# Two expert blocks with per-token heads woven in: first slot's down products summed step by step, bank lanes, heads in quarters, gates as a stage

## The reference, cut to what matters

```python
x = x + _L0_ffn_ref(_layernorm(x, axis=-1), ...)      # experts, first pass (k = 0)
x = x + _L0_attn_b_ref(_layernorm(x, axis=-1), ...)   # heads of one token
x = x + _L0_ffn_ref(_layernorm(x, axis=-1), ...)      # experts, second pass (k = 1)
x = x + _L1_attn_a_ref(_layernorm(x, axis=-1), ...)   # delta rule

# experts: per token the two best of E = 8 experts, one "slot" each
logits = x @ Wg.T
probs = jax.nn.softmax(logits); rw, sel = jax.lax.top_k(probs, K); rw = rw / rw.sum(...)
for k in range(K):                                    # slot k
    x1 = base1 + lora1;  x3 = base3 + lora3           # 896 wide
    x2 = jax.nn.silu(x1) * x3
    down = x2 @ W2.T                                  # beside it a2_all, 256 wide too
    out = out + (down + lora2) * rw[:, k:k + 1]

# heads of one token: 16 heads of 16 numbers, each token for itself
scores = jnp.einsum('bshd,bstd->bsht', q, k) / jnp.sqrt(jnp.float32(HD))
weights = jax.nn.softmax(scores, axis=-1)
attn = jnp.einsum('bsht,bstd->bshd', weights, v)
```

## Time and profile before

| | us |
|---|---|
| median of 3 runs | 1569.86 |
| lowest, highest | 1567.25, 1571.34 |
| the profiled execution | 1570.56 |
| its span | 1568.8 |
| PE busy, share | 1311.2, 84% |
| DVE busy, share | 746.1, 48% |
| ACT busy, share | 419.9, 27% |
| mean granted TensorE clock | 0.89 |

### The profile page before, as it was taken

One profiled execution on the slowest core, in us unless ns is written; L12 is line 12 of the kernel. 1 busy time (PEld: TensorE's weight loads), 2 busy tenths in 40 slices (PEclk: granted clock), 3 DMA queues, 4 the chain that ended last, 5 costly groups with the idle time before them and its releaser, 6 DMA issues.

```text
span 1568.8 us, 17406 instructions
## 1 busy us (share of the span) xinstructions
PE 1311.2 (84%) x6780; PEld 998.9 (64%) x6780; DVE 746.1 (48%) x1631; ACT 419.9 (27%) x910; POOL 79.6 (5%) x69
## 2 busy tenths in 40 slices
PE   5689987986988798877877999879779887897878
PEld 4567563744857678665666766547458576786656
DVE  4533286585445454224233335855943453633241
ACT  2522020111322241334242521111113222413251
POOL 0000000000110110000000000000001102100000
PEclk9889998997999779689987999979979998896898
DMA  9000000000000000000000000000000000000000
GB/s 377 3 1 0 0 1 0 0 1 0 1 1 1 1 1 1 0 1 1 7 8 1 1 0 1 1 0 0 0 0 1 1 0 1 1 1 1 1 1 14
DMA packets 3264, 16.97 MB, mean 11 GB/s; under 512 B 240, under 2 KB 2288, under 8 KB 2544
## 3 DMA queue, kind: packets, MB, share of 16 engines
q10 hardware_dynamic: 1008, 13.77, 2.1%
q1 hardware_dynamic: 2176, 2.10, 0.4%
HBM read 14.82 MB, written 1.05 MB: 10 GB/s over the span
## 4 chain that ended last, share of the span: by engine, by line
PE 61%; DVE 25%; ACT 8%; issue 4%; POOL 1%; DMA 0%; DVEq 0%; ACTq 0%; POOLq 0%
PE bank L612 56%; DVE scr L1657 4%; ACT scr L1167 3%; DVE scr L1658 2%; DVE scr L1641 2%; DVE scr L1640 2%; PE bank L619 2%; DVE scr L1697 1%; PE bank L987 1%; DVE scr L1583 1%; ACT scr L1145 1%; DVE stat L1424 1%; DVE X L1417 1%; DVE scr L1625 1%; POOL rstd L1956 1%
## 5 line engine op out<-in xcount | busy, mean ns | idle before, releaser
L612 PE MATMUL bank<-pack,scr 128*128 128x256 f32 (+2 forms) x944 | 339.1, 515 | 5.2 <-ACT scr L1145 5.2
L612 PE MATMUL bank<-XnT,pack 128*128 128x256 f32 x1024 | 273.6, 412 | 17.7 <-ACT XnT L1145 10.6
L612 PEld LDWEIGHTS bank<-pack,scr 128*128 128x128 f32 x944 | 191.1, 209 | 138.1 <-issue 111.6
L612 PE MATMUL bank<-scr,pack 128*128 128x256 f32 x944 | 242.1, 399 | 30.7 <-DVE scr L1583 25.5
L612 PEld LDWEIGHTS bank<-XnT,pack 128*128 128x128 f32 x1024 | 208.7, 208 | 57.0 <-ACT XnT L1145 13.7
L612 PEld LDWEIGHTS bank<-scr,pack 128*128 128x128 f32 x944 | 186.0, 200 | 63.0 <-DVE scr L1583 28.7
L1145 ACT ACTIVATE scr<-bank 128x512 f32<-128x512 f32 (+7 forms) x112 | 49.0, 454 | 284.6 <-PE bank L619 182.9
L1583 DVE TENSOR_TENSOR scr<-bank,scr 128x256 f32<-128x256 f32 x112 | 45.7, 422 | 165.7 <-ACT scr L1214 165.1
L619 PE MATMUL bank<-pack,scr 128*128 128x128 f32 x232 | 43.1, 319 | 89.1 <-DVE scr L1609 25.0
L1417 DVE TENSOR_TENSOR X<-bank,X 128x512 f32<-128x512 f32 x32 | 22.1, 692 | 185.6 <-PE bank L612 185.5
L612 PE MATMUL bank<-scr 32*128 32x128 f32 (+4 forms) x944 | 101.7, 374 | 8.6 <-DVE scr L1871 4.7
(11 more groups left out here) (175 smaller groups left out, 1462.9 us busy)
## 6 DMA issues: line engine op xcount, KB each, us to landing
pack<-pack_dram ACTq DMA_DIRECT2D x1, 6408.0 KB, 17.9
pack<-pack_dram ACTq DMA_DIRECT2D x1, 2052.0 KB, 30.4
pack<-pack_dram ACTq DMA_DIRECT2D x1, 1595.0 KB, 25.0
pack<-pack_dram ACTq DMA_DIRECT2D x1, 1361.0 KB, 7.4
X<-x SPq DMA_DIRECT2D x4, 256.0 KB, 7.9
pack<-pack_dram ACTq DMA_DIRECT2D x1, 1024.0 KB, 20.0
out_dram<-X SPq DMA_DIRECT2D x4, 256.0 KB, 2.1
pack<-pack_dram ACTq DMA_DIRECT2D x1, 657.5 KB, 26.0
```

Source lines behind the costliest of these rows:

```text
L612: return pe.matmul(o, l, r, start=start, stop=stop, skip_group_check=True)
```

## The change

- **Down sums in the loop.** A new stage `down_sum` stands behind each `x_second` in blocks A and B. It takes the first slot's slice m as soon as it is there and adds its product to two open banks, one for each token half. The `down` stages of slot 0 then issue nothing on PE. In the second slot's `down` the wait for each slice's drained bank stands ahead of that slice's matmul and no longer ahead of all.
- **Bank lanes.** While `weave` is set (from the start of `middle` to the end of block B's `spread`), `x_first` and `down` take banks 0 to 2 only, `down_sum` 3 and 4, all else 5 to 7.
- **Heads in quarters.** `HP = 4`: 16 pieces over 1024 numbers in place of 8 over 2048, in more slots of the loop. `heads_in` and the norm stand one step earlier.
- **Layout of the values.** `bV` is stored with the heads innermost, so that line 1657's multiply reads both operands in a row; ACT's copy writes it so.
- **Gates as a stage.** The gates leave `router` and become a stage of their own behind `spread` or `x_first`; `router` and `lora` move out of the block, `spread_t` stands behind them, and `norm_x` now stands behind `x_first` and `gates`.
- **Convolutions.** In the delta rule two of b's convolution pairs stand one level earlier.

```diff
@@
+HP = 4
...
-            v, o = part(s, o, [NT, NH, HD]); bV.append(v)
+            v, o = part(s, o, [NT, HD, NH]); bV.append(v)
...
             return (pw[s][:, a, hh].unsqueeze(2).broadcast_to([P, n, HD, NH]),
-                    bV[s][:, a].rearrange("p t d -> p d t").unsqueeze(1).broadcast_to([P, n, HD, NH]))
+                    bV[s][:, a].unsqueeze(1).broadcast_to([P, n, HD, NH]))
...
         def lanes(name, k, s):
 
+            if weave[0]:
+                return dict(x_first=range(0, 3), down=range(0, 3), down_sum=range(3, 5)).get(name, range(5, 8))
             if not halves[0]:
...
-            for other in (("scores", 0, (d, 0)), ("spread_t", 0, c), ("spread", 0, c)):
+            for other in (("scores", 0, (d, 0)), ("spread_t", 0, c), ("spread", 0, c), ("gates", 0, c)):
...
         def middle(stage, a, b):
 
+            weave[0] = True
             stage("x_first", 0, (b, 0))
             stage("lora", 0, a)
             stage("norm_x", 2, a)
             experts(stage, 0, b, token_heads(a))
+            stage("router", 1, a)
+            stage("lora", 0, b)
             stage("spread_t", 1, a)
-            stage("lora", 0, b)
             stage("spread", 1, a)
+            stage("x_first", 1, (a, 0))
+            stage("gates", 1, a)
             stage("norm_x", 2, b)
-            stage("x_first", 1, (a, 0))
             experts(stage, 1, a, token_heads(b))
+            stage("router", 1, b)
+            stage("lora", 1, a)
             stage("spread_t", 1, b)
-            stage("lora", 1, a)
             stage("spread", 1, b)
+            weave[0] = False
+            stage("x_first", 1, (b, 0))
+            stage("gates", 1, b)
             stage("norm_x", 4, a)
-            stage("x_first", 1, (b, 0))
...
-                             5: [("norm_t", 4, b), ("delta_gate", 0, b)] + conv_(b, 0),
-                             6: conv_(b, 1) + [("delta_log", 0, b)]})
-            for other in [("delta_u", 0, a)] + conv_(b, 2) + [
-                    ("delta_s", 0, a), ("delta_g1", 0, b), ("delta_v", 0, a), ("delta_tok", 0, b), ("delta_o", 0, a),
+                             5: [("norm_t", 4, b), ("delta_gate", 0, b)] + conv_(b, 0, 1),
+                             6: conv_(b, 2) + [("delta_log", 0, b)]})
+            for other in [
+                    ("delta_u", 0, a), ("delta_s", 0, a), ("delta_g1", 0, b), ("delta_v", 0, a), ("delta_tok", 0, b), ("delta_o", 0, a),
...
-            beside = {1: [("norm_t", 2, s)], 2: [("heads_in", 0, s)] + pieces[0:1]}
-            for i in range(1, 7):
-                beside[2 + i] = pieces[i:i + 1]
-            beside["down00"] = pieces[7:8]
+            beside = {0: [("norm_t", 2, s)], 1: [("heads_in", 0, s)]}
+            slots = [1, "f2", 2, "f3", 3, "f4", 4, "f5", 5, "f6", 6, 7, 7, 8, 8, "down00"]
+            for slot, piece in zip(slots, pieces):
+                beside.setdefault(slot, []).append(piece)
             beside["down10"] = [("head_out_t", 0, s), ("head_out", 0, s), ("norm_x", 3, s)]
-            beside["down11"] = [("norm_t", 3, s), ("router", 1, s)]
+            beside["down11"] = [("norm_t", 3, s)]
...
                     stage("x_second", k, (s, m - 2))
+                    if weave[0]:
+                        stage("down_sum", k, (s, m - 2))
...
+                if ("down", r, i, a) in ring.at:
+                    return
                 o = claim(pe, ("down", r, i, a))
-                if i == 1 and a == 0:
-                    for m in range(FT):
+                for m in range(FT):
+                    if i == 1 and a == 0:
                         wait_drained(pe, ("x", r, m))
...
+            def down_sum(k, sm):
+                s, m = sm
+                r = (k, s)
+                wd = w3("m_down", FT)
+                pe.wait_ge(x2_first[s], nth(s, 2 * FT, k * FT + m + 1))
+                for a in range(NT):
+                    o = claim(pe, ("down", r, 0, a)) if m == 0 else bank[ring.bank(("down", r, 0, a))]
+                    last = mm(o[:, :], x2T[s][:, 0, m, a * P:(a + 1) * P], wd[:, m, :], m == 0, m == FT - 1)
+                    if m == FT - 1:
+                        last.then_inc(full[ring.bank(("down", r, 0, a))], 1)
...
-                move(key, bV[s][:, :, :, :].rearrange("p a h d -> p (a h d)"), psum(key, NT * D))
+                move(key, bV[s][:, :, :, :].rearrange("p a d h -> p a h d"), psum(key, NT, NH, HD))
...
                 ins.then_inc(onehot_ready[s], 1)
 
+            def gates(k, s):
+                iota = w("iota")
                 dve.wait_ge(top_exp[s], nth(s, 2, k + 1))
...
-                hh = slice(h * NH // 2, (h + 1) * NH // 2)
+                hh = slice(h * NH // HP, (h + 1) * NH // HP)
```

32 lines of the change are left out of this document (16 added, 16 removed).

## The result

The changed kernel takes 1586.7 us (median; 1584.9 to 1587.3) against 1569.6 for the kernel before. The ratio is 1.0108, with a 95% interval of 1.0091 to 1.0126: **17 us or 1.1% slower**. The forecast was slower, by 28 us. The profiled execution took 1586.82, with a span of 1585.0 against 1568.8: 16.2 us to account for.

The account below looks back on a forecast made before the run. Blocks A and B were taken as DVE-bound. Block A +8.5, block B +4.6 and ahead of C +1.5 make 14.6 a middle; two give 29.2, less 1.2: +28 us, 1598, own range 1590 to 1606, wide range 1574 to 1616.

Parts of the forecast that it names:

- DVE's waits: Blocks A and B: DVE's waits for ACT's silu or exponential total 14.0 us a block, +9.7 over before.
- The loop's own wait: Slices 3 and 5: x_first needs the bank that DVE's second product of slice m-3 frees; DVE waits 1.7 us.
- the low clock behind it: Slices 4 and 6: PE's 3.6 us idle is followed by a low clock, x_first taking 1.8 us longer.
- clock up (1584): Rival: the 3.6 us idle leaves PE's clock up, 3.6 us less a block, 14.4 in all: 1584, chance 0.16.
- DVE's work: Blocks A and B: quarter pieces, row-wise mix reads and unpaired silu products together change DVE's work by -1.6 us a block.
- H: The start of the head projections on PE in a block; for block B it was to move by -3.5 us.
- A to B: Seam between blocks A and B: x_first of slice 0 ends 5.9 us earlier, norm_t waits 5.4 us; net -3.5 us.
- Ahead of C: Seam ahead of block C: -5.9 us, then +5.2 to norm_t and +2.2 for low clock: +1.5 us.
- Small moves: Elsewhere: earlier maxima and later gates in sequence c's first pass, -1.2 us once; convolution pairs in the delta rule, 0.
- The faster one: Rival: the bank loop doesn't bite, 1559, chance 0.12; the change gains if extra DVE waits stay below 2.7 us a block.
- A clock that swings all through the loop: Rival: x_first of slices 3 and 5 also slow, 1.8 us each, 3.6 a block: 1612, chance 0.10.
- The layout at the full rate: Mix multiply reads bV in a row, 1.22 us a quarter; rival that the layout doesn't help: 1619, chance 0.03.

Follow-up runs that it names:

- layout_alone: The kernel before with only bV stored with its 16 heads in a row, so the mix multiply reads both operands in a row: 1529.6 us.
- exp_later: The changed kernel with ACT's exponential of a token row one piece later in ACT's queue, DVE's order unchanged: 1561.8 us.
- layout_exp_seam: The kernel before with the bV layout, the later exponential, lora_t ahead of router and gates behind x_first 0, norm in its old place: 1489.9 us.

## Why the prediction was right, and where its sizes were off

The direction and the mechanism came as forecast. The size did not: 17 us for 28, and 1586.7 lies in the wide range but outside the forecast's own, 1590 to 1606.

**The bound.** Right. Blocks A and B hang on DVE; shortening DVE's work by 5.37 us shortens the stretch by 5.37 us in all four (layout_alone).

**DVE's waits.** The loop was right, and it was the point on which the forecast turned. The forecast's waits add up to 14.0 us a block; 14.1, 13.0, 13.0 and 14.0 were measured. The loop's own wait was put at 1.7 and is 1.91; PE's idle ahead of slices 4 and 6 was put at 3.6 and is 3.46, all eight times. **The term of these stretches that was mis-sized is the low clock behind it**: I took 1.8 us in all eight cases, from the row behind 3.90 us of idle. It came in four, and added 2.8, 1.7, 1.7 and 2.8 us to the waits: 9.0 us where the sum had 14.4. That the waits of a block fit so well is partly luck: without the clock they are 11.3 us where I had 10.5, which takes back 3.2 of those 5.4. And that 1587 lies between my two cases, clock low (1598) and clock up (1584), isn't owed to the half of low clocks alone. It moves the forecast by 5.4 us, to 1593; the rest came from places outside the loop.

**DVE's work.** Put at -1.6 us a block. From H to the end the blocks grew by 7.9, 6.8, 6.8 and 7.8 us for 8.1; less the added waits as measured that leaves -1.8. A quarter operation is 1.22 us, as worked out.

**The seams.** A to B: the way from the last normalization of A to H of B was to shrink by 3.5 us, and went from 43.9 to 40.3 and from 47.6 to 43.4, 3.6 and 4.2. `x_first` of slice 0 was to end 5.9 us earlier and ends 5.3 earlier (counted from `norm_t` 3, first seam): the idle ahead of `lora_t` fell to 1.32 us as worked out, but half of this `x_first` still ran at the low clock. The wait of `norm_t`, put at 5.4, is 5.26; the two rows ahead of and behind it:

```profile
291.96 0.42 DVE L1609 TENSOR_TENSOR scr<-bank,scr 128x256 f32<-128x256 f32 x1 [4.19 <-ACT scr L1238]
...
295.84 0.86 DVE L1456 TENSOR_SCALAR scr<-X,mv,rstd 128x256 f32<-128x256 f32 x2 [0.81 <-POOL rstd L1982]
```

```profile
296.76 1.12 PE L630 MATMUL bank<-pack,scr 128*128 128x128 f32 x4 [5.26 <-DVE scr L1456]
```

Ahead of C I had +1.5 twice; the first gave +1.2, the second -1.4. There the kernel before had run an `x_first` at a low clock and the changed one only its first half, which I had seen but left out of the sum.

**Small moves.** c's region gained 2.8 us for 1.2; the gates' 5.56 us stood ahead of more than the scores' maxima. I haven't taken that apart. The delta rule was put at 0. The idle ahead of `delta_base`'s level went as weighed up (5.89 us to 2.65 and 0.57), the masks' wait came (3.87 us), and they cancel to 0.8 us; but behind it b's delta rule ran at the low clock for 20.5 us where it had been 27.3, which is 3.4 us less, and **no term stood for it**: the whole stretch up to c's router gave 4.8 us where I had put nothing. What turned the clock there I haven't taken apart.

**The sum.** The blocks and seams gave 21.9 for 29.2 (DVE's waits and work 3.0 less, the seams 0.8, C 3.2), c 1.6 less, the delta rules and the rest 2.9 less: 11.8 us, which is 28 less 16.2. So three quarters of the miss lie outside the stretches that the forecast turned on.

**The rivals.** The faster one, decided at 2.7 us of extra waits a block, was far off: the extra waits were 8.6 to 9.7. "A clock that swings all through the loop" had the Trainium skill's page "TensorE: Matmul & The Clock Gate" (section "A second HAM failure mode: psum-queue depth-cycling") behind it; no run shows it: behind the idles of 0.4 to 0.9 us at slices 3 and 5, and of 1.19 us at 4 and 6 in exp_later, the clock never fell. My own ground against it was weak, though: the idle of 4.4 us lies as far back from 284.70, where the clock was up, as from 1172.06, where it was low. The layout at the full rate, for which the Trainium skill's page "SBUF — State Buffer" (section "Door 1: The DMA port swizzle") stood, came: 1.22 us for a quarter and 2.29 for a half, where the old stride took 1.90 and 3.63.

What the forecast did not see is the size of what was on offer: it priced the layout at 5.4 us a block, as work of DVE, and not that PE's idle at the tail goes with it. In the changed kernel that doesn't matter, since the idle stays. It did in every better version.

## What to carry over

Before cutting the banks of a stage into lanes, follow the ring once around: which engine frees the bank, what stands in its queue ahead of the freeing instruction, and whether that engine then waits for what the bank lets start; a fourth bank, or a larger piece between two visits, opens the loop. Move work to the engine's idle place, not away from it, and look at the idle behind the stretch as well as in it, as the clock is paid there. And an instruction with slack (here an exponential that is read several slots later) does not belong ahead of one that another engine waits for: moved one slot back, it gave 4.5 us a block at no cost (layout_exp_seam against layout_alone).
